# Attention row maxima two banks at a time, scores in three single banks, exponentials of 512 columns, values behind an odd tile's scores

## The reference

```python
Q = heads(layernorm(x) @ Wq + bq); K = heads(ctx @ Wk + bk); V = heads(ctx @ Wv + bv)
A = softmax(scale * Q @ K.T)          # 512 queries x 1024 keys, per head and batch
x = x + tanh(g) * ((A @ V) @ Wo + bo)
```

## Time and profile before

| | us |
|---|---|
| three runs | 1052.80, 1053.20, 1059.21 |
| their median | 1053.2 |
| span of the profiled execution (first to last instruction) | 1052.7 |

### The profile page before, as it was taken

The page is one execution under the profiler, slowest core; times in us unless marked ns, Lnnn a source line. Parts: engine busy times, 40 slices in busy tenths (PEclk is TensorE's granted clock), DMA queues, the critical chain, the costliest instruction groups (busy, mean ns, idle before and its releaser), DMA issues.

```text
span 1052.7 us, 17430 instructions
## 1 busy us (share of the span) xinstructions
PE 971.8 (92%) x6530; PEld 574.6 (55%) x6530; DVE 774.0 (74%) x1445; ACT 488.9 (46%) x708; POOL 290.5 (28%) x439
## 2 busy tenths in 40 slices
PE   8897987999999977999689999999999999899998
PEld 4333353444444454999254444445788788644446
DVE  4989888999999631454489899995664645699956
ACT  2672331477777721121027777776312212347763
POOL 3656710133343203002302433322500400013230
PEclk9998989999999977999899999999999999999999
DMA  6889912103320323995341233201254242110001
GB/s 205 271 266 311 361 35 69 43 25 115 124 86 23 98 85 115 327 374 186 90 150 47 63 84 83 62 9 42 87 192 141 84 140 100 28 45 13 8 2 40
DMA packets 79181, 121.81 MB, mean 116 GB/s; under 512 B 9733, under 2 KB 52904, under 8 KB 79090
## 3 DMA queue, kind: packets, MB, share of 16 engines
q1 hardware_dynamic: 59278, 79.29, 24.3%
q10 hardware_dynamic: 19044, 39.22, 10.7%
q0 software_dynamic: 768, 2.10, 0.6%
HBM read 92.10 MB, written 27.81 MB: 114 GB/s over the span
## 4 chain that ended last, share of the span: by engine, by line
PE 67%; DVE 20%; DMA 5%; issue 3%; ACT 2%; POOL 2%; SPq 0%; DVEq 0%; ACTq 0%; POOLq 0%
PE bank L1601 15%; PE bank L1567 15%; PE bank L1822 12%; DVE arena L2343 10%; PE st_bank L1752 4%; PE bank L1764 4%; DMA kparts<-arena 3%; PE st_bank L1586 3%; PE st_bank L1822 2%; PE bank L1361 2%; PE st_bank L1515 1%; PE bank L1655 1%; PE bank L1620 1%; DVE bnst L1925 1%; PE st_bank L1891 1%
## 5 line engine op out<-in xcount | busy, mean ns | idle before, releaser
L2343 DVE TENSOR_REDUCE arena<-bank 128x1 f32<-128x512 f32 x640 | 397.1, 681 | 33.7 <-PE bank L1567 32.8
L1208 ACT ACTIVATE arena<-st_bank 128x1024 f32<-128x1024 f32 x320 | 312.3, 1022 | 137.1 <-PE st_bank L1586 136.0
L1567 PE MATMUL bank<-g_a 64*128 64x512 f32 x480 | 181.5, 477 | 11.7 <-DVE arena L2343 3.3
L1601 PE MATMUL bank<-arena,vaug 128*9 128x256 f32 (+2 forms) x2560 | 168.5, 381 | 1.3 <-ACT arena L1208 1.3
L1567 PEld LDWEIGHTS bank<-g_a 64*128 64x128 f32 x480 | 73.2, 183 | 124.9 <-DVE arena L2343 100.3
L1822 PE MATMUL bank<-g_a,g_w 128*128 128x512 f32 x512 | 117.3, 390 | 1.1 <-POOL g_a L959 1.1
L1586 PE MATMUL st_bank<-g_a 64*128 64x512 f32 x480 | 115.3, 417 | 0.0
L1822 PEld LDWEIGHTS bank<-g_a,g_w 128*128 128x128 f32 x512 | 95.9, 188 | 21.9 <-POOL g_a L959 2.0
L926 POOL COPY arena<-arena 8x32 f32<-8x32 f32 x160 | 34.8, 217 | 259.4 <-issue 137.2
L1601 PEld LDWEIGHTS bank<-arena,vaug 128*9 128x9 f32 (+2 forms) x2560 | 55.8, 92 | 75.2 <-issue 39.7
L1567 PE MATMUL bank<-g_x,g_a 64*128 64x512 f32 x160 | 63.4, 494 | 9.6 <-DVE arena L2343 3.5
(11 more groups left out here) (329 smaller groups left out, 1442.3 us busy)
## 6 DMA issues: line engine op xcount, KB each, us to landing
arena<-in_glu_w SPq DMA_DIRECT2D x39, 512.0 KB, 3.2
arena<-kv_table SPq DMA_DIRECT2D x11, 1024.0 KB, 7.6
ctxT<-in_glu_w ACTq DMA_DIRECT2D x22, 512.0 KB, 5.9
arena<-in_w SPq DMA_DIRECT2D x20, 512.0 KB, 5.9
kparts<-arena ACTq DMA_DIRECT2D x12, 512.0 KB, 5.4
arena<-in_w ACTq DMA_DIRECT2D x12, 512.0 KB, 3.4
xnT<-kv_table SPq DMA_DIRECT2D x5, 1024.0 KB, 8.0
g_a<-kparts SPq DMA_DIRECT2D x24, 192.0 KB
```

The lines of the kernel that those rows point to most:

```text
L1208: act.activation(prob[sl % PROBS], st_bank[sl % 2][:], ACT.Exp, scale=scale).then_inc(exp_ready, 1)
L1567: pe.matmul(bank[TURN_BANKS[place % 3]], Qc[gi % KQ_BUFS][rows, qt * P:(qt + 1) * P], Kc[gi % KQ_BUFS][rows, half * CH:(half + 1) * CH], s ...
L1601: ins = pe.matmul(bank[7][at:at + dh + 1, 0:D], vaug[l][:, b * KT + 2 * m + i, h0 + hh, :], tiles[:, a], start=(m == 0 and i == 0), stop=( ...
L2343: dve.tensor_reduce(mxh[gi % 2][:, col, hf:hf + 1], bank[TURN_BANKS[place % 3]], AX.X, ALU.max).then_inc(max_red, 1)
```

## The change

Four things are done together.

- **Banks.** The eight PSUM banks are given out anew: banks 0 to 2 are a ring for the scores (`SCORE_BANKS`), banks 3 to 6 are two pairs for the maxima (`max_pair`), bank 7 stays with the values.
- **Maxima.** A step now makes one pair: both heads of one query tile and one half of the keys, in two banks side by side, and one reduction of 128x1024 to 128x2 reads both. There are 320 reductions in place of 640. PE fills a pair when the reduction two pairs before is done.
- **Scores and exponentials.** Each of the two heads' products of a tile is one unit of the ring, waits for its own bank (`ring_bank`: the unit three before has been read), and has its own exponential of 512 columns: 640 in place of 320. Turning the context takes one unit of the ring instead of a bank of the maxima's rotation.
- **Order.** With pairs, the order of a cycle is: a pair, scores of the even tile, a pair, scores of the odd tile, values. The values follow the odd tile's scores at once.

Small things follow from the new banks: the queries' product takes banks 0, 1, 2, 1 (the fourth waits until bank 1 has been read), late tokens are turned into other banks, the waits on `st_mm` count twice as far, and the filler, output and last context products start from the maxima's banks when their last reduction is done.

```diff
     def maxima(upto):
         nonlocal u
         while u < min(upto, total):
-            turn("max", u)
-            u += 1
-            if u in LATE[l]:
-                steps.append(LATE[l][u])
+            steps.append(("max", u))
+            u += HG
+            steps.extend(LATE[l][v] for v in (u - 1, u) if v in LATE[l])
...
-            maxima(LEAD + HG * sl - sl % 2)
+            maxima(LEAD + HG * sl)
...
-            steps.append(("score", g, kt))
-            maxima(LEAD + HG * sl)
-            if sl % 2 and sl >= VALUES_LAG:
-                steps.append(("values", (sl - VALUES_LAG) // KT, (sl - VALUES_LAG) % KT // 2))
+            steps.append(("score", g, kt, ring))
+            ring += HG
+            scored[sl] = ring
+            if sl % 2 and valued + VALUES_LAG <= sl:
+                values()
...
             if kt == CTX_SLOT and g and g % 2 == 0:
-                context(g - 1)
+                steps.append(("turned", g - 1, ring))
+                ring += 1
+                steps.append(("normal", g - 1, ring))
...
-        st_bank = [ctx.enter_context(nc.psum_tensor(f"st_bank{i}", [P, 2, CH], F32)) for i in range(2)]
-        bank = [st_bank[i // 2][:, i % 2, :] for i in range(4)]
-        bank += [ctx.enter_context(nc.psum_tensor(f"bank{i}", [P, CH], F32))[:, :] for i in range(4, 8)]
+        st_bank = ctx.enter_context(nc.psum_tensor("st_bank", [P, SCORE_BANKS, CH], F32))
+        max_bank = ctx.enter_context(nc.psum_tensor("max_bank", [P, 2 * HG, CH], F32))
+        value_bank = ctx.enter_context(nc.psum_tensor("value_bank", [P, CH], F32))
+        bank = [st_bank[:, i, :] for i in range(SCORE_BANKS)] + [max_bank[:, i, :] for i in range(2 * HG)] + [value_bank[:, :]]
+        max_pair = [max_bank[:, 0:2, :], max_bank[:, 2:4, :]]
...
-                        act.wait_ge(st_mm, sl + 1)
-                        act.activation(prob[sl % PROBS], st_bank[sl % 2][:], ACT.Exp, scale=scale).then_inc(exp_ready, 1)
+                        for hh in range(HG):
+                            act.wait_ge(st_mm, HG * sl + hh + 1)
+                            act.activation(prob[sl % PROBS][:, hh, :], bank[(r + hh) % SCORE_BANKS], ACT.Exp, scale=scale).then_inc(exp_ready, 1)
...
+                    if p >= len(max_pair):
+                        pe.wait_ge(max_red, GROUP0[l] * PAIRS + p - len(max_pair) + 1)
...
+                def ring_bank(r):
+                    if r >= SCORE_BANKS:
+                        pe.wait_ge(exp_ready, RING0[l] + r - SCORE_BANKS + 1)
+                    return bank[r % SCORE_BANKS]
...
-                    if sl >= 2:
-                        pe.wait_ge(exp_ready, sl - 1)
                     for hh in range(HG):
                         rows = slice(hh * HALF_P, (hh + 1) * HALF_P)
-                        ins = pe.matmul(st_bank[sl % 2][:, hh, :], Kc[gi % KQ_BUFS][rows, kt * P:(kt + 1) * P], Qc[gi % KQ_BUFS][rows, :], start=True, stop=True)
-                    ins.then_inc(st_mm, 1)
...
+                        pe.matmul(ring_bank(r + hh), Kc[gi % KQ_BUFS][rows, kt * P:(kt + 1) * P], Qc[gi % KQ_BUFS][rows, :], start=True, stop=True).then_inc(st_mm, 1)
...
-                    dve.tensor_reduce(mxh[gi % 2][:, col, hf:hf + 1], bank[TURN_BANKS[place % 3]], AX.X, ALU.max).then_inc(max_red, 1)
+                    dve.tensor_reduce(mxh[gi % 2][:, qt:qt + QT + 1:QT, half], max_pair[(p + FIRST_PAIR[l]) % len(max_pair)], AX.X, ALU.max).then_inc(max_red, 1)
```

More of the change, by code:

```diff
@@ L57 @@
 QCH0 = {l: sum(EC[i] * T // CH for i in range(1, l)) for l in range(1, 5)}
+RING0 = {l: sum(HG * KT * NGROUPS[i] + NGROUPS[i] // 2 - 1 for i in range(1, l)) for l in range(1, 5)}
 GEN_STEPS = M // WIN - 1
@@ L100 @@
 TURN_BANKS = (4, 5, 6)
+PAIRS = HALVES // HG
+SCORE_BANKS = 3
+QUERY_BANKS = (0, 1, 2, 1)
+FIRST_PAIR = {1: 0, 2: 1, 3: 0}
 NORMAL_LAG = 4
@@ L163, in maxima, with values @@
         while u < min(upto, total):
-            turn("max", u)
-            u += 1
-            if u in LATE[l]:
-                steps.append(LATE[l][u])
+            steps.append(("max", u))
+            u += HG
+            steps.extend(LATE[l][v] for v in (u - 1, u) if v in LATE[l])
             if u % HALVES == 0:
                 steps.append(("shift", u // HALVES - 1))
-            if WARM_FROM <= u <= LEAD and u % HG == 0:
+            if WARM_FROM <= u <= LEAD:
                 steps.append(("warm",))
-    def context(g):
-        turn("context", g)
-        steps.append(("normal", *steps[-1][1:]))
+    valued, ring, scored = 0, 0, {}
+    def values():
+        nonlocal valued
+        steps.append(("values", valued // KT, valued % KT // 2, scored[valued + 1]))
+        valued += 2
     for g in range(NGROUPS[l]):
@@ L203, in schedule @@
         first_gate(0)
-    steps += [("values", NGROUPS[l] - 1, m) for m in range((KT - VALUES_LAG + 1) // 2, KT // 2)]
+    while valued < NGROUPS[l] * KT:
+        values()
     if l == 3:
@@ L207, in schedule @@
     steps.append(("copy", NGROUPS[l] - 1))
-    context(NGROUPS[l] - 1)
+    turn("context", NGROUPS[l] - 1)
+    steps.append(("normal", *steps[-1][1:]))
     if l == 3:
@@ L218, in schedule @@
         turn("out", (B - 1, i))
+    assert ring == RING0[l + 1] - RING0[l]
     return steps
@@ L1193, in attention @@
                             q_store(l, QCH0[l] + j, 1)
-                    elif step[0] == "normal" and step[1] < NGROUPS[l] - 1:
-                        _, g, place = step
+                    elif step[0] == "turned":
+                        _, g, r = step
                         k = (GROUP0[l] + g) // 2
@@ L1533, in attention @@
                 order = schedule(l)
-                rotation = [step for step in order if step[0] in ("max", "context", "heads", "out", "hold", "mix tokens", "mix")]
+                rotation = [step for step in order if step[0] in ("context", "heads", "out", "hold", "mix tokens", "mix")]
                 def bank_read(place):
+                    if place < len(TURN_BANKS):
+                        return max_red, GROUP0[l + 1] * PAIRS
                     step = rotation[place - len(TURN_BANKS)]
@@ L1562, in row_max @@
                         pe.wait_ge(kq_ld[gi % KQ_BUFS], keys_and_queries(gi))
-                    if place >= len(TURN_BANKS):
-                        pe.wait_ge(*bank_read(place))
-                    elif l == 3 and TURN_BANKS[place] == 6:
-                        pe.wait_ge(x_ready, stage * NT - 1)
-                    pe.matmul(bank[TURN_BANKS[place % 3]], Qc[gi % KQ_BUFS][rows, qt * P:(qt + 1) * P], Kc[gi % KQ_BUFS][rows, half * CH:(half + 1) * CH],
-                              start=True, stop=True).then_inc(max_mm, 1)
+                    if p >= len(max_pair):
+                        pe.wait_ge(max_red, GROUP0[l] * PAIRS + p - len(max_pair) + 1)
+                    elif l == 2 and p == 1:
+                        pe.wait_ge(xnT_ready, (LN_AT[stage] + 1) * 4)
+                    elif l == 3 and p == 1:
+                        pe.wait_ge(x_ready, stage * NT - 1)
+                    for hh in range(HG):
+                        rows = slice(hh * HALF_P, (hh + 1) * HALF_P)
+                        ins = pe.matmul(max_pair[(p + FIRST_PAIR[l]) % len(max_pair)][:, hh, :], Qc[gi % KQ_BUFS][rows, qt * P:(qt + 1) * P], Kc[gi % KQ_BUFS][rows, half * CH:(half + 1) * CH],
+                                        start=True, stop=True)
+                    ins.then_inc(max_mm, 1)
                 def hold_bank(place):
@@ L1611, in warm, with turn_pair @@
                             pe.matmul(out, eye, bc(eye.unsqueeze(1), [HALF_P, D // P, P]), start=True, stop=True)
-                def turn_context(g, place):
-                    gi = GROUP0[l] + g
-                    pe.wait_ge(pv_evac, gi + 1)
-                    pe.wait_ge(*bank_read(place))
-                    turned = bank[TURN_BANKS[place % 3]].rearrange("p (t r e) -> p t r e", t=QT, r=2)
+                def turn_pair(g, out):
+                    turned = out.rearrange("p (t r e) -> p t r e", t=QT, r=2)
                     for i in range(2):
```

82 lines of the change are left out of this document (43 added, 39 removed).

## The result

| | before | after |
|---|---|---|
| median, lowest and highest of four runs, us | 1053.11 (1052.80 to 1059.21) | 1081.12 (1079.25 to 1081.47) |
| span of the profiled execution, us | 1052.7 | 1079.7 |
| PE / VectorE / ScalarE busy, us | 971.8 / 774.0 / 488.9 | 971.2 / 753.9 / 509.0 |

The changed kernel takes 1.0243 times as long, with an interval of 1.0218 to 1.0268: 28 us more. All engines together are as busy as before. VectorE has 20 us less to do, ScalarE 20 us more, PE the same. What grew is waiting.

A forecast was written before the change was run, and what follows sets the result against it. No single engine bounds the kernel, but a 2.68 us loop of values, maxima and a reduction; the change makes a 2.88 us loop through ScalarE. 20.7 + 9 - 2 = +27.7 on 1052.7, plus 0.5 around it, gives 1081 us, range 1045 to 1098.

The forecast's parts named there:

- The loop (+20.7): Cycles with maxima beside them: three banks for four score units make a cycle 2.88 us, not 2.68; +20.7 us over 139 cycles.
- All six links: Values 0.98, maxima pair to score 0.34, score to exponential 0.50, exponential 0.60, ScalarE to PE 0.04, waiting score to values 0.42.
- Both bounds on the unknown links: Score-to-exponential and exponential times: low ends give a 2.67 us loop and 1045 us, a 0.69 exponential gives 2.97 and 1098.
- The turned cycle: Cycle with the turned context: the last score unit waits for a second exponential, 0.50 us more than the 2.88 cycle.
- The tail (+9): Seven cycles behind each layer's last maxima: the score loop adds 3.8, 3 and 2 us in layers 1, 2 and 3.
- values to exponential, 360.10 to 361.81, 1.71: Layer 1's filler cycle behind the maxima: 1.71 us, then 0.60 + 0.04 + 0.42, makes 2.77 against 1.99, +0.8.
- The lead (-2): The 28 maxima at each layer's start: less VectorE work, part hidden by the late layer norm, -2 us in all.
- 28 x 0.60 to 14 x 1.14, 0.8 us a layer: VectorE's reductions in each layer's lead: 14 pairs at 1.14 us replace 28 maxima at 0.60, 0.8 us less a layer.
- one of the prediction's signs of being wrong: Stated signs: a 2.4 us cycle with VectorE full, the waiting score starting at once, or a lead differing over 3 us a layer.
- The first, that engines set the pace (998): Faster rival: no wait on the score ring, cycle 2.41 us against 2.79, 998 us in all; chance 0.13.
- The second (2.67 to 2.70): No-change rival: the score loop comes out as long as the old one, 1045 to 1063 us, middle 1054; chance 0.19.
- The third, a falling clock: Slower rival: PE idle 0.46 us a cycle lowers the clock to 1.2 GHz in a tenth of cycles, +16, 1097 us; chance 0.10.

The follow-up runs named there:

- the late pair: Changed kernel with the odd tile's pair of maxima behind its scores and the values behind that pair: 1114.69 us, 1.0543 of before.
- the best kernel made here: Changed kernel with values halved, one tile's behind each tile's scores, and one pair of maxima moved ahead of each group's first half: 1028.9 us, 0.9737 of before.
- the kernel with the moved pair: Changed kernel with the even tile's pair of maxima behind its scores instead of ahead of them: 1050.73 us, 0.9967 of before.

## Why the prediction was right

1081 us was predicted and 1081.12 measured. The closeness is partly luck: two terms were off by 2 and 4.4 us in opposite directions, and 2.5 us lie outside the attention's stretches.

**The loop (+20.7): right, in mechanism and in size.** All six links came out as taken: 0.98, 0.33, 0.49, 0.61, 0.04, 0.43 against 0.98, 0.34, 0.50, 0.60, 0.04, 0.42. The exponential of 512 columns is 602 ns, and the pair's reduction follows another every 1.14, as worked out from the 1024-column row. Both bounds on the unknown links turned out to be wider than needed. The runs show the loop from each side: shortening its exponential shortens the cycle one for one, shortening the reduction does nothing, taking the pair out from ahead of a0 shortens it, a pair behind b1 makes it longer, and halving the values ends it. In the kernel with the short exponentials, four score banks and the old order it does not arise. VectorE idles as said, 0.52 us a cycle. The turned cycle is 3.36 to 3.37 where 3.38 was taken.

**The tail (+9): right mechanism, mis-sized, +11.0.** By layers it is 3.9, 3.8 and 3.3 us. Layer 1, the one that was worked out, came out as the sum said, 3.8. What was too small are the 3 and 2 that were taken for layers 2 and 3, "whose tails have more other products": those products hide less of the loop than was thought. In layer 1 every term is near. The first cycle is 1.90 from the last pair to the values, as predicted. Behind the output product it is 0.57 longer where 0.4 was taken, and three filler cycles are 2.4 longer, as taken. The last filler cycle lost 0.57 and the end of the layer gained 0.65, two that were left at nothing. One link of the filler cycle was too short all the same, "values to exponential, 360.10 to 361.81, 1.71". In that row both scores of a tile start together behind the fillers. Now fillers and scores alternate one by one in the trace:

```profile
371.60 1.05 PE L1619 MATMUL value_bank<-arena,vaug 128*9 128x256 f32 x16
372.59 0.39 PE L1589 MATMUL max_bank<-identb 64*128 64x512 bf16 x1
372.60 0.50 PE L1605 MATMUL st_bank<-g_a 64*128 64x512 f32 x1
...
373.51 2.06 ACT L1219 ACTIVATE arena<-st_bank 128x512 f32<-128x512 f32 x4 [0.92 <-PE st_bank L1605]
...
374.59 1.05 PE L1619 MATMUL value_bank<-arena,vaug 128*9 128x256 f32 x16
```

From values to exponential it is 373.51 - 371.60 = 1.91, and the cycle 2.99 against the 2.77 of the sum. Other filler cycles of this layer are 2.65 and 2.77, and the old ones were slower than the 1.99 taken, up to 2.20, so that the difference came out right.

**The lead (-2): right sign, mis-sized, -6.4.** The step "28 x 0.60 to 14 x 1.14, 0.8 us a layer" is mis-sized in two ways. First, the first score does not wait for all of these reductions. It starts while the 26th of 28 runs before, and while the 13th of 14 runs after, and up to there VectorE spends 1.2 us less a layer on them, 3.5 in all. Second, VectorE idles 2.7 us less in the leads, 3.6 for 6.3, which the step left out. In layer 1 VectorE's rows before, where each bracket is a wait:

```profile
182.13 2.48 DVE L2343 TENSOR_REDUCE arena<-bank 128x1 f32<-128x512 f32 x4 [0.24 <-PE bank L1567]
...
186.84 0.69 DVE L2343 TENSOR_REDUCE arena<-bank 128x1 f32<-128x512 f32 x1 [0.65 <-PE bank L1567]
```

and after, five pairs in a row without one:

```profile
182.16 5.97 DVE L2368 TENSOR_REDUCE arena<-max_bank 128x2 f32<-128x1024 f32 x5
...
188.30 1.23 DVE L2368 TENSOR_REDUCE arena<-max_bank 128x2 f32<-128x1024 f32 x1 [0.17 <-PE max_bank L1582]
```

That VectorE has more in store with four banks for the maxima, when late parts of the norm and of the queries hold PE up, fits these rows, but it is not shown: no run gave the maxima three banks again, and in layer 2 the idle time did not fall at all (2.1 and 2.3). Most of the gain in idle time is layer 3's, 2.8 to 0.6, and it is not steady: with the late pair, whose lead is the same, layer 3's lead idles 2.5. This layer's lead is 3.7 us shorter than before, so one of the prediction's signs of being wrong, a lead that differs by more than 3 us in a layer, did come up.

**The rivals.** The first, that engines set the pace (998), fell: the loop was there. But even without the loop its 2.41 was not reached. With the values split the cycle is 2.45 without a turned context, and the copy of the value bank takes its part; the best kernel made here is 1028.9. The second (2.67 to 2.70) fell too; its cycle is near that of the kernel with the moved pair, but for another reason. The third, a falling clock, fell too: from 200 to 250 us the changed kernel has PE busy 45.97 of 50, less than the 48.83 of before, as the rival said, and its clock is still 1.00, as in the earlier trace rows. The mean over the whole execution is 0.970 and was 0.969. Of all kernels run, only the slowest, with the late pair, shows a lower one in that stretch:

```profile
200.00:250.00 50.00, 42.58 (x381) 18.14 (x373) 39.91 (x39) 33.20 (x66) 13.56 (x34) 0.97 0.08 25
```

**The two rules weighed.** The rule of breaking instructions up (the Trainium skill, Perfetto Trace Analysis, Optimizing Scalar/DVE Operations) asks that ScalarE hold others up. Breaking the exponentials up was tried by itself, in the kernel before: 0.9997, neither gain nor loss. There ScalarE is not in the loop, so the rule's condition was not met and the run does not speak against it. In the changed kernel it is met, and no run puts the exponentials of 1024 back. The rule of rotating banks (the Trainium skill, the same page, Optimizing Tensor Performance, Matmuls) is the one that this kernel turned on: the trace agrees, with 0.29 us of PE and 0.52 of VectorE idle in the cycle shown, whose fourth unit finds no bank.

## What to carry to other kernels

When banks are given out anew, count the units that pass through each ring between two things that cannot overtake each other in PE's queue, here the values. If there are more units than banks, the loop is: block, unit, latency, its reader, latency, the waiting unit; add its links up, and compare with the busiest engine's share of the cycle before counting any gain of that engine. Such a loop can be shortened for nothing by order: put the first unit right behind the block and all independent work between it and the unit that waits (here 29 us in the steady stretches). Cut the block to end the loop, looking first at what then comes closer together. And look for the wait on the weight loads' rows: a chain that names one engine alone can still be a loop through another.

## What I had not expected

- Work in the loop is paid for, but not by its full width: a pair of products took 0.34 from start to start in the stream and added 0.23, ahead of a0 as behind b1, and nothing between the two.
- Halving a block brings its halves closer together: ScalarE's copy of the value bank cost nothing while a cycle lay between two blocks of values, and 0.43 us a group once only half a cycle did.
- PE idle in every cycle left the granted clock where it was: 1.00 from 200 to 250 us with 45.97 of 50 busy. In the slowest kernel it was 0.97 there, by one fall to 1.2 GHz around 200 us; from 210 to 250 us, with 8.16 to 8.82 of each 10 us busy, it was 1.00 again. What made it fall is not shown.
